# Weighted sum of the cross-attention in one PSUM bank: 21 short matmuls a turn in place of 15, and a third bank for the maxima

## What is computed

```python
x = x + xattn(_layernorm(x), ctx)          # x: 32 x 56 x 128, ctx: 32 x 1500 x 64, four times
scores = einsum('bqhd,bkhd->bhqk', Q, K) * scale
attn = softmax(scores, axis=-1)            # over the 1500 rows of the context
O = einsum('bhqk,bkhd->bqhd', attn, V)     # then the output projection
```

## Time and profile before

| | |
|---|---|
| median of 3 runs | 4039.97 us (4037.01 to 4041.73) |
| span of the profiled execution | 4037.7 us; no time beside its span is given for it |
| TensorE busy | 94% of the span, 43467 matmuls |
| VectorE, ScalarE, GpSimd busy | 78%, 66%, 63% |
| mean granted TensorE clock | 0.954 |
| TensorE in the chain that ended last | 87% |

### The profile page before, as it was taken

The page is one execution under the profiler, slowest core; times in us unless marked ns, Lnnn a source line. Parts: engine busy times, 40 slices in busy tenths (PEclk is TensorE's granted clock), DMA queues, the critical chain, the costliest instruction groups (busy, mean ns, idle before and its releaser), DMA issues.

```text
span 4037.7 us, 110587 instructions
## 1 busy us (share of the span) xinstructions
PE 3793.1 (94%) x43467; PEld 2886.6 (71%) x43467; DVE 3135.7 (78%) x6499; ACT 2674.0 (66%) x5365; POOL 2544.9 (63%) x2457
## 2 busy tenths in 40 slices
PE   6999999989969999999799999996997899999987
PEld 4777777766637777777577777775765677777765
DVE  6999999858978888888577888886654788888864
ACT  4888887756637777777467777773442577777752
POOL 4888888759856776767456676675001476676761
PEclk8999999979989999999699999998998899999988
DMA  4333333125432222121112212110000212122100
GB/s 129 104 110 112 110 108 107 41 92 158 143 100 61 57 60 61 54 61 49 28 54 62 59 54 64 57 54 21 3 1 18 64 54 64 57 59 61 55 22 15
DMA packets 157328, 266.80 MB, mean 66 GB/s; under 512 B 26632, under 2 KB 97432, under 8 KB 155432
## 3 DMA queue, kind: packets, MB, share of 16 engines
q1 hardware_dynamic: 156360, 259.67, 22.5%
q10 hardware_dynamic: 448, 0.06, 0.0%
HBM read 165.10 MB, written 50.26 MB: 53 GB/s over the span
## 4 chain that ended last, share of the span: by engine, by line
PE 87%; DVE 6%; POOL 2%; ACT 2%; DMA 1%; issue 1%; SPq 1%; POOLq 0%; DVEq 0%; ACTq 0%
PE ps L186 83%; PE ps L659 1%; DVE xn L166 1%; POOL wst L539 1%; PE ps L242 1%; PE ps L255 1%; PE ps L1638 1%; DVE wst L817 1%; DVE wst L772 0%; PE ps L1160 0%; DVE st L151 0%; DMA big<-big 0%; DVE relu L769 0%; DMA ynN<-cx 0%; ACT wb L324 0%
## 5 line engine op out<-in xcount | busy, mean ns | idle before, releaser
L539 POOL TENSOR_TENSOR wst<-wst 125x384 bf16<-125x384 f32 (+1 forms) x1536 | 1432.0, 932 | 843.4 <-ACT wst L745 783.1
L745 ACT ACTIVATE wst<-ps 125x448 f32<-125x448 f32 x3072 | 1518.5, 553 | 569.3 <-PE ps L186 554.8
L186 PE MATMUL ps<-big,cx 128*125 128x448 bf16 (+1 forms) x6144 | 1428.8, 354 | 0.8 <-DMA big<-topT 0.8
L186 PEld LDWEIGHTS ps<-cx,wst 125*128 125x128 bf16 x23040 | 1113.5, 98 | 307.5 <-POOL wst L539 15.2
L817 DVE TENSOR_TENSOR wst<-wst 125x512 bf16<-125x512 f32 (+1 forms) x1536 | 1269.4, 827 | 56.8 <-ACT wst L745 56.5
L186 PE MATMUL ps<-cx,wst 125*128 125x65 bf16 (+2 forms) x23040 | 1202.4, 204 | 12.1 <-POOL wst L539 11.6
L186 PEld LDWEIGHTS ps<-big,cx 128*125 128x125 bf16 (+1 forms) x6144 | 835.1, 137 | 284.2 <-issue 1.8
L186 PE MATMUL ps<-cx,big 128*128 128x500 bf16 (+1 forms) x2688 | 709.4, 317 | 10.2 <-DVE big L1743 2.6
L772 DVE TENSOR_REDUCE wst<-ps 128x1 f32<-128x500 f32 x896 | 603.9, 674 | 136.6 <-PE ps L186 123.9
L769 DVE CUSTOM_DVE_ANT_0 wst<-ps,wst 128x500 bf16<-128x500 f32 x448 | 302.6, 676 | 207.2 <-PE ps L186 150.8
L769 DVE CUSTOM_DVE_ANT_0 relu<-ps,relu 128x500 bf16<-128x500 f32 x448 | 301.8, 674 | 147.8 <-PE ps L186 84.1
(11 more groups left out here) (250 smaller groups left out, 4260.2 us busy)
## 6 DMA issues: line engine op xcount, KB each, us to landing
big<-big SPq DMA_DIRECT2D x768, 56.0 KB, 2.7
cx<-ctxT SPq DMA_DIRECT2D x96, 375.0 KB, 3.5
cx<-ctxN SPq DMA_DIRECT2D x64, 377.9 KB
cx<-in_ctxN SPq DMA_DIRECT2D x64, 375.0 KB
cx<-ctxT SPq DMA_DIRECT2D x96, 187.5 KB, 3.8
ctxN<-cx SPq DMA_DIRECT2D x32, 377.9 KB
ynN<-cx SPq DMA_DIRECT2D x32, 377.9 KB
cx<-ynN SPq DMA_DIRECT2D x32, 377.9 KB
```

The source lines that it names most:

```text
L186: return t.matmul(o, l, r, start=start, stop=stop, skip_group_check=True)
L539: g.tensor_tensor(pl[r][0:KP, at:], pf[r][0:KP, at:], pf[r][0:KP, at:].bitcast(BF16)[:, 1::2], ALU.subtract).then_inc(s["plp"], 1)
L745: e.activation(pf[T % 3][0:KP, cols], bank(2 + n2 % 3, 448)[0:KP], ACT.Exp, scale=scale).then_inc(s["ev"], 1)
```

## The change

For every block `j` the matmul of 129 columns becomes two, of 65 and of 64 columns, and the second accumulates into the same 64 columns as the first. So the sum over high and low part of the context is made in PSUM; the result has 65 columns a block, 455 in all, and fits into bank 5 (`ACC` = 2560). The number of columns that stream through TensorE in a turn stays 1358. ScalarE copies once instead of twice, the addition of the two parts goes away on GpSimd (L546) and, for the last item, on VectorE (L801), and GpSimd's steps of the finish stand at other turns. Bank 6 becomes a third one for the maxima.

```diff
-        raw = [wst[:, 4032 + 903 * i:4935 + 903 * i].rearrange("p (j c) -> p j c", j=NJ) for i in range(2)]
+        raw = [wst[:, 4032 + 455 * i:4487 + 455 * i].rearrange("p (j c) -> p j c", j=NJ) for i in range(2)]
...
-            return n % 2 if k else ORDER.index(item) % 4
+            return (0, 1, 6)[n % 3] if k else ORDER.index(item) % 4
...
-            b4, of = (kb, ORDER[n - (2 if k else 4)]) if n >= 2 else (kb - 1, ORDER[n - 2])
-            if k == 1 and n < 2:
+            back = 3 if k else 4
+            b4, of = (kb, ORDER[n - back]) if n >= back else (kb - 1, ORDER[n - back])
+            if k == 1 and n < 3:
                 w.wait_ge(s["red"], maxima(kb, ORDER[0]))
...
-                if 0 <= (k := due(T, KT + 4)) < B - 1:
-                    u, kb = k % 2, B * ci + k
-                    r = raw[u][:, :, 0:C]
-                    w.wait_ge(s["fc"], 2 * (kb + 1))
-                    g.tensor_tensor(r, r, raw[u][:, :, C + 1:], ALU.add).then_inc(s["fp"], 1)
-                    w.wait_ge(s["fp"], 4 * kb + 1)
-                if 0 <= (k := due(T, KT + 7)) < B - 1:
+                if 0 <= (k := due(T, KT + 5)) < B - 1:
...
-                if 0 <= (k := due(T, KT + 8)) < B - 1:
+                if 0 <= (k := due(T, KT + 7)) < B - 1:
...
-                if 0 <= (k := due(T, KT + 10)) < B - 1:
+                if 0 <= (k := due(T, KT + 9)) < B - 1:
...
-                    if k:
-                        w.wait_ge(s["fc"], 2 * (b0 + k) - 1)
+                    w.wait_ge(s["fc"], b0 + k)
                     for j in range(NJ):
-                        if k and j == 3:
-                            w.wait_ge(s["fc"], 2 * (b0 + k))
...
-                        at = 2620 + 129 * j
-                        n = min(129, 3072 - at) if at < 3072 else 129
-                        mm(t, ps[:, at:at + n], ph[:, cols], cnb[k % 3][:, i, 0:n], i == 0 and j == 0, False)
-                        if n < 129:
-                            mm(t, ps[:, at + n:at + 129], ph[:, cols], cnb[k % 3][:, i, n:129], i == 0, False)
+                        at = ACC + 65 * j
+                        mm(t, ps[:, at:at + 65], ph[:, cols], cnb[k % 3][:, i, 0:C + 1], i == 0 and j == 0, False)
+                        mm(t, ps[:, at:at + C], ph[:, cols], cnb[k % 3][:, i, C + 1:], False, False)
                         r_ = mm(t, ps[:, at:at + 65], pl[r][0:KP, cols], cnb[k % 3][:, i, 0:65], False, i == KT - 1)
...
-                    e.activation(whole[:, 0:452], ps[:, 2620:3072], ACT.Copy).then_inc(s["fc"], 1)
-                    e.activation(whole[:, 452:], ps[:, 3072:2620 + 129 * NJ], ACT.Copy).then_inc(s["fc"], 1)
+                    e.activation(whole, ps[:, ACC:ACC + 65 * NJ], ACT.Copy).then_inc(s["fc"], 1)
...
-                        v.tensor_tensor(r, r, raw[u][:, :, C + 1:], ALU.add).then_inc(s["fp"], 1)
                         w.wait_ge(s["rd"], kb + 1)
-                        w.wait_ge(s["fp"], 4 * kb + 1)
                         v.tensor_tensor(r, r, per_row(rden[u][:, :], C), ALU.mult).then_inc(s["fp"], 1)
```

More of the change, by code:

```diff
@@ L23 @@
 EPS = 1e-5
+ACC = 2560
 TWICE = 6
@@ L552, in pool_cross @@
                     g.tensor_tensor(r, r, per_row(rden[u][:, :], C), ALU.mult).then_inc(s["fp"], 1)
-                    w.wait_ge(s["fp"], 4 * kb + 2)
-                if 0 <= (k := due(T, KT + 8)) < B - 1:
+                    w.wait_ge(s["fp"], 3 * kb + 1)
+                if 0 <= (k := due(T, KT + 7)) < B - 1:
                     u, kb = k % 2, B * ci + k
@@ L559, in pool_cross @@
                     g.tensor_copy(O[:, k % HB, :, 0:C], r).then_inc(s["fp"], 1)
-                    w.wait_ge(s["fp"], 4 * kb + 3)
-                if 0 <= (k := due(T, KT + 10)) < B - 1:
+                    w.wait_ge(s["fp"], 3 * kb + 2)
+                if 0 <= (k := due(T, KT + 9)) < B - 1:
                     u, kb = k % 2, B * ci + k
@@ L564, in pool_cross @@
                     g.tensor_tensor(O[:, k % HB, :, C:], r, O[:, k % HB, :, 0:C], ALU.subtract).then_inc(s["fp"], 1)
-                    w.wait_ge(s["fp"], 4 * kb + 4)
+                    w.wait_ge(s["fp"], 3 * kb + 3)
         def pe_cross(t, w, ci, xh_, xl_, biased=False):
@@ L656, in pe_cross @@
                 if what == "turn":
-                    w.wait_ge(s["fp"], 4 * (b0 + k + 1))
+                    w.wait_ge(s["fp"], 3 * (b0 + k + 1))
                     for j in range(NJ):
@@ L721, in act_cross @@
                     if k >= 2:
-                        w.wait_ge(s["fp"], 4 * (kb - 1))
+                        w.wait_ge(s["fp"], 3 * (kb - 1))
                     whole = raw[k % 2].rearrange("p j c -> p (j c)")
-                    e.activation(whole[:, 0:452], ps[:, 2620:3072], ACT.Copy).then_inc(s["fc"], 1)
-                    e.activation(whole[:, 452:], ps[:, 3072:2620 + 129 * NJ], ACT.Copy).then_inc(s["fc"], 1)
+                    e.activation(whole, ps[:, ACC:ACC + 65 * NJ], ACT.Copy).then_inc(s["fc"], 1)
                 what, p, k = slot(T)
@@ L794, in dve_cross @@
                 if (k := due(T, KT + 3)) >= 0:
-                    w.wait_ge(s["fc"], 2 * (b0 + k + 1))
+                    w.wait_ge(s["fc"], b0 + k + 1)
                     v.reciprocal(rden[k % 2][:, :], raw[k % 2][:, :, C]).then_inc(s["rd"], 1)
@@ L799, in dve_cross @@
                         r = raw[u][:, :, 0:C]
-                        w.wait_ge(s["fp"], 4 * kb)
-                        v.tensor_tensor(r, r, raw[u][:, :, C + 1:], ALU.add).then_inc(s["fp"], 1)
+                        w.wait_ge(s["fp"], 3 * kb)
                         w.wait_ge(s["rd"], kb + 1)
-                        w.wait_ge(s["fp"], 4 * kb + 1)
                         v.tensor_tensor(r, r, per_row(rden[u][:, :], C), ALU.mult).then_inc(s["fp"], 1)
-                        w.wait_ge(s["fp"], 4 * kb + 2)
+                        w.wait_ge(s["fp"], 3 * kb + 1)
                         w.wait_ge(s["otr"], kb - HB + 1)
                         v.tensor_copy(O[:, k % HB, :, 0:C], r).then_inc(s["fp"], 1)
-                        w.wait_ge(s["fp"], 4 * kb + 3)
+                        w.wait_ge(s["fp"], 3 * kb + 2)
                         v.tensor_tensor(O[:, k % HB, :, C:], r, O[:, k % HB, :, 0:C], ALU.subtract).then_inc(s["fp"], 1)
```

## The result

| | before | after |
|---|---|---|
| median of 4 runs | 4040.72 us (4037.01 to 4041.73) | 4059.26 us (4054.06 to 4061.21) |
| span of the profiled execution | 4037.7 us | 4052.2 us (its time 4054.06) |

The change makes the kernel 0.47% slower, ratio 1.0047, interval 1.0032 to 1.0061. The medians are 18.5 us apart, the spans 14.5; the profiled execution after the change is the fastest of its four.

What follows compares the result with a forecast made beforehand. TensorE alone was taken to bound the steady part. Added matmuls +28, heads -6, tails -4 and GpSimd's waits -4 gave +14 us, laid on the median of 4040: 4054 us, 8-in-10 range 4018 to 4082.

Steps and rivals of the forecast that it cites:

- 9216 matmuls on TensorE: Steady part: six more matmuls a turn at 3 ns each, +28 us, bounds from -10 to +55.
- heads, third bank: Layer heads: products wait for the reader three back, 1.8 us less in layers 1 to 3, 0.8 in layer 0; -6 us.
- tails, copy and add: Last item's finish: second copy and add go, 0.4 + 0.6 = 1.0 us a layer, -4 us.
- GpSimd's waits: Tails: TensorE's waits for GpSimd's `pl`, 11.6 us, lose a third through earlier finish steps; -4 us, between 0 and -8.
- The three readings: Cost per matmul above its columns: layer 2's bias 2.3 ns, all 594 matmuls 3.6, weighted sum 3.6 with projections 2.5.
- The rule on weight loads: Skill's rule: a load of 128 columns takes 107 ns, some 53 fast; binding loads would give 4404 us, chance 2%.
- The rival of dear accumulation or two right operands in quick order: Weighted sum: these cost 6 ns a matmul and more, time 4081 us and above; chance 12%.
- The first rival: Steady part: short matmuls cost only what their columns cost, time 4026 us, down to 4014; chance 20%.
- it cancels: Rival: 1 to 2.2 ns a matmul, gains as forecast or somewhat larger, time 4032 to 4048 us; chance 22%.
- the third bank does nothing: Rival on the heads: they end as late as before, time 4060 us; 15% within the forecast's own range.

Runs made afterwards that it cites:

- e3: The kernel before with only its matmuls of 129 split into 65 and 64, each into columns of its own over two banks: 4079.31 us, ratio 1.0095.
- e4: The kernel after with two banks instead of three for the maxima of items 1 and up: 4067.62 us, ratio 1.0065.
- e6: The kernel after with GpSimd's three finish steps back at turns 7, 8 and 10 instead of 5, 7 and 9: 4066.18 us, ratio 1.0061.
- e9: The kernel after with `cnb` rows of 136 columns instead of 129, low parts from column 72: 4032.85 us, ratio 0.9978.
- e5: The kernel after with `cnb` rows of 130 columns, low parts from column 66: 4049.55 us, ratio 1.0022.
- e12: The kernel after with `cnb` rows of 132 columns, low parts from column 68: 4043.86 us, ratio 1.0004.
- e13: The kernel after with `cnb` rows of 138 columns, low parts from column 72: 4040.93 us, ratio 0.9997.
- e10: e9 with the seven results 72 columns apart in PSUM instead of 65, copied with a stride: 4030.75 us, ratio 0.9973.
- e7: The kernel after with `cnb` rows of 160 columns, low parts from column 96: 4038.17 us, ratio 0.9991.
- e1: The kernel after with `cnb` rows of 130, a zero column at the end, and the middle matmul of each triple 65 wide: 4070.22 us, ratio 1.0075.
- e2: The kernel after with the low-parts matmul of the context moved from second to third in its block: 4059.49 us, ratio 1.0047.

## Why the prediction was right, and what was off in it

The forecast was +14 us on the span (4054), the measured span rose by 14.5 and the median by 18.5 (4059). Direction and mechanism hold, and the bound in three of the four layers. The cost was forecast 12 us too low and the gains 7 to 8 too low, so that they nearly cancelled: how near the total came is luck.

| term | forecast | measured | by |
|---|---|---|---|
| 9216 matmuls on TensorE | +28 | +45 by the period of layers 1 to 3, +41 with layer 0, +40 by medians | period, stretches, e3 |
| heads, third bank | -6 | -9 | e4 |
| tails, copy and add | -4 | -5 | last row of the table of stretches |
| GpSimd's waits | -4 | -7 to -8 | e6 |
| sum | +14 | +18 to +19, with the 40 | +18.5 by the medians |

*What bounds it.* Right for layers 1 to 3: the steady chain is TensorE alone in both kernels, and the 324 us less on GpSimd and ScalarE show nowhere there, as forecast with the cover named. The forecast read two items of layer 1 and laid that on all 1536 turns. In layer 0 of the kernel before VectorE is in the steady chain, and the period is 46.28 us; there the change costs 0.44 us a period in place of 0.71, 4 us less over 16 periods. The split alone does it: in e3 VectorE is out of this chain too, at 46.77. So part of the longer turns of TensorE was hidden behind a wait that the forecast took to be absent.

*The steady part* is the term that was mis-sized most: 3 ns a matmul, measured 4.9. The three readings averaged over matmuls of all kinds, or took matmuls of 56 columns, whose operands lie otherwise. What the split of a 129 of `cnb` costs stood in the trace of before, in block 3: by single starts its two parts take 30 + 33 = 63 ns, where the 129 columns of the other six take 56 to 60, 58 in the mean. That is 5 ns, the measured price. The forecast drew from block 3 only that its group was no longer than 620 ns.

The Trainium skill, "TensorE: Matmul & The Clock Gate", section "Wait — 56ns, not 53.3ns?", gives a fixed cost of about 2.5 ns for each warm matmul above its columns. By that figure the change would be +23 us, an estimate. The trace agrees for the 65-column matmuls (29 ns for 27.1) and the projections (26 for 23.3), and not for the 64-column ones (33 for 26.7); there the measurement decides. The rule on weight loads that the forecast set aside is set aside by the runs too: 21 pairs in 646 ns are 31 ns a pair.

*The rival of dear accumulation or two right operands in quick order* named the right place (`cnb` begins at rows of 129) with the wrong price and joined to a wrong cause. Accumulation is cleared by e3, the change of right operand as such by e9, which has as many changes and 28 ns behind the low parts; where the low parts begin is what counts, by e5, e9, e12 and e13. The price, 4.9 ns, stays below its 6.

*The first rival*, that only columns count, fell as the forecast said it would: the period rose by 0.71. With the operands moved (e9, e10) the period is 46.41 and 46.34, 0.36 and 0.29 over before: 2.5 and 2.0 ns a matmul, which is the case "it cancels", and these kernels end at 4033 and 4031 us.

*The heads.* Layer 1 went as replayed, 4.54 us for a forecast of 4.5. What the forecast left out is that the bank also helps in the 48 turns behind. Layer 0 was given 0.8 us; its head reads 2.9 shorter after, but in the nine other kernels with three banks it takes 17.7 to 20.5, against 19.9 to 20.4 with two, and its first 48 turns are 3.7 longer, while the wait for the maxima's DMA rose from 0.8 to 2.1 us. Together I read nothing from it that is the bank's. That the third bank does nothing is refuted by e4.

*Tails.* The last stretch fell by 1.65, 1.44, 1.29 and 0.78 us, 5.2 in all, for 4.0. No experiment takes the copy and the add back alone. TensorE's wait for the last item's low part fell from 13.4 to 9.7 us over four layers, 0.9 each.

*GpSimd.* A third of the waits was to go; 8.0 of 11.6 went. e6, with the add gone and the old turns, has 10.1: 6.5 of the 8.0 come with the turns, 1.5 are left for the add.

**Open.** Why about every fourth short matmul still takes 4 ns more where no low parts are dear: not PSUM's place (e10 only moved it); the weights' places were not varied. Whether low parts that begin earlier than their row, but not at a multiple of 16, are cheap: no layout had them. And e7 and e13 end 5 and 8 us behind e9, e7 at the same period and e13 at one 0.06 us longer (4 us); that was not followed up.

## What to carry to other kernels

Where TensorE bounds, count matmuls as well as columns, and read the price of one more from single start times of the very operands that it will use, not from a group's mean. Before splitting a matmul, see where in memory the right operands of the parts begin, and give them the same place within 16 bytes: here padding rows of 129 to 136 was worth 21 to 26 us of 4059 and turned a loss of 0.47% into a gain of 0.22% (0.27% with e10). Moves that only relax waits at the head and tail of a stage are worth their few microseconds each, and an experiment that takes back one at a time shows them when the sum hides them.

## What was not expected of the hardware

- Two right operands in turn, some 65 columns each: when the second begins later within 16 bytes than the first, the next start comes 33 to 34 ns behind it, at the same place or a multiple of 16 after 28 to 29 (medians over blocks; two blocks of e10 have 32). Neither one column more (e1) nor the third place in the triple (e2) changes that. Some 4 to 6 of 21 gaps are long even then.
- Accumulating into columns that the matmul just before wrote costs nothing that shows: 646 ns a group with it (after) and without (e3).
- The same GpSimd instructions stall TensorE for 10.1 us at one set of turns and 3.6 at another.
